# Eight buffers in place of four for the gathered token tiles of the last layer

## The reference, cut to what matters

```python
xf = x.reshape(B * T, D)                  # 4096 tokens, D = 128
logits = xf @ gate_W.T                    # 8 experts
pi = _sinkhorn(-logits)                   # 20 rounds over rows and columns
_, top_idx = jax.lax.top_k(pi, 2)
g = jnp.einsum('nd,efd->enf', xf, W_gate)     # f = 512
u = jnp.einsum('nd,efd->enf', xf, W_up)
y = jnp.einsum('enf,edf->end', jax.nn.silu(g) * u, W_down)
out = sum over k of y[top_idx[:, k], n] * pi[:, k:k + 1]
x = _layernorm(x + out)
```

## Time and profile before

| | us |
|---|---|
| median of 3 runs | 2434.86 (2433.98 to 2436.57) |
| the profiled execution | 2434.3 |
| its span, first to last instruction | 2432.5 |
| TensorE busy | 1741.1 (72%) |
| VectorE busy | 1712.0 (70%) |
| ScalarE busy | 941.0 (39%) |
| GpSimd busy | 803.8 (33%) |

### The profile page before, as it was taken

One profiled execution on the slowest core, in us unless ns is written; L12 is line 12 of the kernel. 1 busy time (PEld: TensorE's weight loads), 2 busy tenths in 40 slices (PEclk: granted clock), 3 DMA queues, 4 the chain that ended last, 5 costly groups with the idle time before them and its releaser, 6 DMA issues. The chain is left out here.

```text
span 2432.5 us, 29879 instructions
## 1 busy us (share of the span) xinstructions
PE 1741.1 (72%) x9233; PEld 1061.5 (44%) x9233; DVE 1712.0 (70%) x3432; ACT 941.0 (39%) x1424; POOL 803.8 (33%) x773
## 2 busy tenths in 40 slices
PE   6999965655589947777877877679997221788880
PEld 3555554654556612322322332256666110455550
DVE  4999966677668828888888889869995567333326
ACT  2444431122144446456446545345553221222230
POOL 2222211222110025666566556532220000344441
PEclk9999987777789968888878888989997555899995
DMA  4000000000000000000000000000002200011113
GB/s 119 1 0 0 1 11 6 0 5 0 0 1 0 0 9 1 1 1 1 0 0 0 0 0 1 0 9 6 5 3 76 106 1 0 24 33 33 33 31 107
DMA packets 38099, 38.05 MB, mean 16 GB/s; under 512 B 7261, under 2 KB 32965, under 8 KB 37493
## 3 DMA queue, kind: packets, MB, share of 16 engines
q1 hardware_dynamic: 33461, 27.60, 3.7%
q0 software_dynamic: 4544, 9.32, 1.3%
HBM read 25.69 MB, written 11.21 MB: 15 GB/s over the span
## 5 line engine op out<-in xcount | busy, mean ns | idle before, releaser
L1498 PE MATMUL PS<-m_hC,identf 128*128 128x512 f32 x512 | 331.9, 735 | 146.4 <-POOL m_hC L1256 140.8
L1256 POOL TENSOR_TENSOR m_hC<-m_h,m_Cs 128x512 f32<-128x512 f32 x256 | 337.6, 1327 | 227.5 <-DVE m_h L1391 150.4
L1391 DVE TENSOR_TENSOR_SCAN m_h<-m_dA,PS 128x512 f32<-128x512 f32 x256 | 312.4, 1220 | 30.4 <-ACT m_dA L1344 19.5
L1498 PEld LDWEIGHTS PS<-m_hC,identf 128*128 128x128 f32 x512 | 102.2, 224 | 289.8 <-POOL m_hC L1256 264.2
L1386 DVE TENSOR_TENSOR PS<-PS,m_DU 128x512 f32<-128x512 f32 x256 | 178.4, 697 | 31.7 <-PE PS L1471 19.1
L1344 ACT ACTIVATE m_dA<-m_DT,m_A 128x508 f32<-128x508 f32 x256 | 178.2, 716 | 25.2 <-DVE m_h L1391 23.9
L1349 ACT COPY m_Cs<-PS 128x512 f32<-128x512 f32 x128 | 74.4, 581 | 273.6 <-PE PS L1478 273.6
L1629 POOL DMA_INDIRECT e_XG<-token_rows,e_ids x71 | 69.2, 974 | 237.0 <-DVE e_ids L1770 215.7
L82 POOL TENSOR_TENSOR ln_lv<-ln_mv,ln_eps 128x4 f32<-128x4 f32 x40 | 8.1, 202 | 361.2 <-DVE ln_mv L75 361.2
L1783 DVE TENSOR_TENSOR e_H<-PS,e_Sg 128x512 f32<-128x512 f32 x71 | 49.1, 692 | 108.9 <-PE PS L1872 99.5
L1675 ACT ACTIVATE e_Sg<-PS 128x512 f32<-128x512 f32 x71 | 42.4, 598 | 195.9 <-PE PS L1871 189.5
(11 more groups left out here) (347 smaller groups left out, 4110.7 us busy)
## 6 DMA issues: line engine op xcount, KB each, us to landing
token_rows<-X SPq DMA_DIRECT2D x2, 2048.0 KB, 12.2
e_Y<-expert_rows SPq DMA_DIRECT2D x16, 256.0 KB, 3.7
e_w_wg<-in_w_wg SPq DMA_DIRECT2D x1, 2048.0 KB, 8.0
e_w_wu<-in_w_wu SPq DMA_DIRECT2D x1, 2048.0 KB, 12.4
e_w_wd<-in_w_wd SPq DMA_DIRECT2D x1, 2048.0 KB, 16.9
out_dram<-X SPq DMA_DIRECT2D x8, 256.0 KB, 2.3
X<-in_x SPq DMA_DIRECT2D x1, 1792.0 KB, 7.5
x_Cs<-in_ctx SPq DMA_DIRECT2D x8, 154.0 KB
```

The costliest lines, as they stand in the source:

```text
L1256: nc.gpsimd.tensor_tensor(hC[:, i % ND, :], hst[:, i % ND, :], Cs[:, n % ND, :], ALU.mult).then_inc(s["hC"], 1)
L1391: nc.vector.tensor_tensor_scan(hst[:, i % ND, :], dA[:, i % ND].rearrange("p b l -> p (b l)"), bank(4), 0.0, ALU.mult, ALU.add).then_inc(s ...
L1498: nc.tensor.matmul(bank(5 + ch), c.identf[:, :], hC[:, i % ND, :], start=(n == 0), stop=(n == NS - 1)).then_inc(s["yacc"], 1)
```

## The change

The gathered tiles get a ring of their own, RG = 8 buffers with eight semaphores; RB = 4 stays for the scatters, for the reloaded rows and for the layout of the DRAM tensors. GpSimd issues eight gathers ahead, and in the loop the gather of tile i+8 ahead of the scatter of tile i. The tile Acc, of 4 KB a partition, is no longer allocated: its name is now a view of XL, which has the same size and is used at the head of the phase alone. XG grows by 2 KB a partition.

```diff
-    RB = 4
+    RB, RG = 4, 8
...
-    gs = list(c.sems("e_", " ".join(f"g{i}" for i in range(RB))).values())
+    gs = list(c.sems("e_", " ".join(f"g{i}" for i in range(RG))).values())
...
-    XG = sb("XG", [P, RB, D])
+    XG = sb("XG", [P, RG, D])
...
-    Acc = sb("Acc", [P, 2, GB, D])
+    Acc = XL[:, :, :].rearrange("p i (b d) -> p i b d", b=GB)
...
             def gather(i):
-                if i >= RB:
-                    pool.wait_ge(s["xT"], i - RB + 1)
-                nc.gpsimd.indirect_dma_start(out=XG[:, i % RB, :], out_offset=None, in_=XD[:, :],
-                                             in_offset=bass.IndirectOffsetOnAxis(ap=ids[:, i:i + 1], axis=0)).then_inc(gs[i % RB], 16)
+                if i >= RG:
+                    pool.wait_ge(s["xT"], i - RG + 1)
+                nc.gpsimd.indirect_dma_start(out=XG[:, i % RG, :], out_offset=None, in_=XD[:, :],
+                                             in_offset=bass.IndirectOffsetOnAxis(ap=ids[:, i:i + 1], axis=0)).then_inc(gs[i % RG], 16)
...
-            for i in range(RB):
+            for i in range(RG):
                 gather(i)
             for i in range(NT):
-                if i + RB < NT:
-                    gather(i + RB)
+                if i + RG < NT:
+                    gather(i + RG)
                 scatter(i)
...
             def x_transposed(i):
-                pe.wait_ge(gs[i % RB], landed(i))
+                pe.wait_ge(gs[i % RG], 16 * (i // RG + 1))
                 if i:
                     pe.wait_ge(s["xTc"], i)
-                nc.tensor.transpose(PS[:, XTB, 0:P], XG[:, i % RB, :], c.identf[:, :]).then_inc(s["xT"], 1)
+                nc.tensor.transpose(PS[:, XTB, 0:P], XG[:, i % RG, :], c.identf[:, :]).then_inc(s["xT"], 1)
```

## The result

| | before | after |
|---|---|---|
| median, us | 2434.76 (2433.98 to 2436.57, 4 runs) | 2377.93 (2376.53 to 2378.55, 4 runs) |
| profiled execution, us | 2434.3 | 2378.2 |
| its span, us | 2432.5 | 2376.4 |
| first transposition of the loop, us | 2084.24 | 2085.31 |
| transpositions of tiles 4 to 70, us | 267.77 | 210.43 |

The ratio is 0.9765, 95% interval 0.9748 to 0.9782. The forecast was 2375.6 us in a range of 2372 to 2391.

A forecast was written before the change was run, and what follows sets the result against it. Bound: gathers queued behind scatters in GpSimd's queue, 4.057 us a tile; eight buffers leave TensorE's 3.16. Span 2432.5 - 59.2 = 2373.3 us, 2375.1 as profiled execution, 2375.6 as median; range 2372 to 2391.

The forecast's parts named there:

- The closed chain through GpSimd's queue: Tile loop: gather(i+4) stands behind scatter(i-1), which waits for TensorE's iteration i+2; a turn of 8.06 us carries two tiles.
- The count, RG - 2: Tile loop: tiles carried by one 8.06 us turn; two with four gather buffers, six with eight, 1.34 us a tile.
- The step of 3.16 us: Tile loop: TensorE's unwaited time a tile becomes the bound; 66 steps take 208.56 us, a gain of 59.2 us.
- Start: Head of the loop: four further gathers, 5.1 us, fit into GpSimd's idle 8.85 us before the first scatter; no cost.
- end: From the last transposition to the end of the span: 69.0 us, moved forward by the gain with its length kept.
- alias: Acc as a view of XL: zero cost, with 1.2 us allowed both ways for tiles at other addresses.
- semaphores: Four more semaphores, cleared once at the end: 0 to 1.2 us, taken as 0.
- Slow starts: Rival: TensorE's iterations keep 3.36 us a tile, 13.2 us more, 2388.8 us in all; chance 0.09.
- No effect by a slow landing: Rival: gathers are late by their landing, not their issue, so more buffers don't help; 2434.9 us, chance 0.03.
- GpSimd as bound: Rival at gather and scatter issue: slower past 4.06 us a tile; at twice the issue durations 2465 us; chance 0.03.
- The clock: TensorE's granted clock stays at 1.00 when fuller, as at 729.6 to 851.2 us; no case of its own.
- my two cases: Forecast for three gather buffers: about 2699 us, or about 2930 us if the clock falls to its lower level in the waits.

The follow-up runs named there:

- The first profile: The changed kernel unaltered, its first profiled execution: 210.43 us from tile 4 to tile 70, span 2376.4 us.
- the second: The changed kernel unaltered, profiled once more: 208.69 us from tile 4 to tile 70, span 2376.3 us.
- the kernel with a quarter of down: Changed kernel with one block of four left of the down projection, H's transpositions and ScalarE's HT copy: 2327.70 us (one run).

## Why the prediction was right

**What bounds.** The closed chain through GpSimd's queue was the cause, and it was shown from both sides: undone by the order alone with four buffers (2377.97 us), undone by the fifth buffer (2378.39), and made worse by taking the fourth away (2849.32).

**The count, RG - 2.** Right at three (one tile a turn) and at four (two); at five and eight TensorE takes over, as forecast, and hides the count. The pair of steps read in the earlier trace rows, 3.36 and 4.70 us, fits 40 of the 66 steps or so; in the other 26, most of them of 3.7 to 4.3 us, both tiles of a turn wait, which is why there are 46 waits in some 33 turns. The sum over two tiles is the same, so the forecast doesn't depend on it. The prediction could have gone one step on: five buffers suffice, and so does another order.

**The step of 3.16 us.** Read from one pair of transpositions, it held over the whole loop: 3.158 where nothing is late. The gain in the loop was put at 59.2 us. The first profile shows 267.77 - 210.43 = 57.3, the second 59.1. The term that I left out is the late copies, up to 2 us. The last transposition came at 2307.34, where 2304 had been forecast.

**Start, end, alias, semaphores.** The further gathers were free (gap 3.86 us left), the tail is 69.1 us for 69.0, the alias measures 1.0003. The loop began 1.07 us later than in the profile of before, for a reason that is not in the change: over the executions profiled, all with the same code ahead of the loop, the first transposition came between 2084.1 and 2087.0 us (2088.1 with each gather issued twice, where it waits for two issues). Loop, start and end make up the span: 57.3 - 1.1 - 0.1 = 56.1 us. The miss of 2.3 us against the forecast is these two, about 1.9 and 1.1, with the spread of the runs. That split holds for the first profile only: in the second the loop lost next to nothing, but began at 2087.02, and the run took 2378.14 us, as long as the first. Both terms differ by 2 to 3 us between executions and were not in the sum; that they came out small beside the gain is no merit of the forecast.

**The rivals.** Slow starts (3.36 a step): none, from the fourth tile on each start but one records 0.27 as the unwaited ones did before (the one, 0.30, stands behind the latest of the late copies). No effect by a slow landing: out. GpSimd as bound: its place and its price (3.81 us a tile for 3.84, with each gather twice) were right, and it is the next bound behind TensorE; but at 2.57 us a tile it stays under TensorE's 3.16. The issues' means stay at 945 to 989 ns while VectorE's share rises from 31% to 37% (40% had been forecast), and to 47% in the kernel with a quarter of down. The rule of the Trainium skill (SBUF — State Buffer, Who interferes with whom) on the port pair that GpSimd and VectorE share had a part in that rival; no run here shows it at work where VectorE reads PSUM.

**The clock** stayed at 1.00, as in the stretch chosen for comparison. That a loop with waits of 0.2 to 1.6 us holds its clock says nothing on one with waits of 4.5 us; there my two cases were both wrong, and the measured time lay between.

## What to carry to other kernels

In a queue that issues loads ahead and stores behind, ask of each load behind which store it stands, and at which iteration of the slowest engine that store can go: the prefetch depth that counts is the ring less the length of that detour, here 8 - 2 or 4 - 2. If a load waits for a store that has nothing to do with its buffer, moving the store back in the queue can be worth as much as doubling the ring, as it was here, and costs no memory. Compute the next bound at once, as a duration per tile of each engine: it says how much of added depth can pay (here the first buffer of four).

## What was not expected of the hardware

A loop whose TensorE waits 4.5 us in each 10.2 us ran at a mean granted clock of 0.67, with both levels inside one iteration: gate and up at 1.2 GHz, down at 2.4 GHz. The same loop with four buffers, its 46 waits 0.2 to 1.6 us long, had 1.00. The missing buffer was so paid twice: with the longer wait, and with 2.2 us more for the work behind it.

In some executions VectorE's copies of the down projection start about 1 us late, two of them over 2 us, though nothing but the down projection holds them: they stand right behind TensorE's signal, which comes late while TensorE's own next instructions keep nearly their pace. Why it does is open. A wait that seems to be for a DMA can so be one for an engine; the releaser in the timeline's rows tells.

The landing of an indirect scatter of 64 KB to DRAM is 2.2 to 3.4 us, median 2.3 (in the kernel with a quarter of down), hardly different from the gather's 2.4 to 3.7, median 2.6, in the kernel before. The Trainium skill (DMA: Bandwidth & Descriptors, Anatomy of one DMA) gives a fixed 2.0 us or so and the bytes at 436 GB/s on top, by which 64 KB would take 2.15 us, an estimate, and lays most of it to the confirmation of the last write. The medians here agree with the estimate to within 0.15 and 0.45 us; how the time divides no run here shows.
